# An attention and mixture-of-experts kernel: gate weights of the last token block moved from VectorE to GpSimd, and the waits of the first scatter-adds of each list put in another order

## The reference

```python
x = x + moe(layernorm(x))
# moe(h), h: 2048 x 256, 8 experts of width 512, the two best for each token
probs = softmax(h @ wg.T)
topk_w, topk_idx = top_k(probs, 2)
topk_w = topk_w / sum(topk_w)
y_e = (silu(h @ w1[e].T) * (h @ w3[e].T)) @ w2[e].T     # for each expert e
out = sum over the token's two experts of topk_w * y_e
```

## Time and profile before

| | us |
|---|---|
| median of 3 runs | 520.24 (519.79 to 520.38) |
| the profiled execution | 518.94 |
| its span, first to last instruction | 517.2 |
| TensorE busy | 497.2 (96%) |
| VectorE busy | 378.0 (73%) |
| ScalarE busy | 286.7 (55%) |
| GpSimd busy | 278.1 (54%) |

### The profile page before, as it was taken

How to read it: one execution, slowest core, us unless ns; L and a number is a source line. 1 busy time by engine, 2 the same in 40 slices (tenths; PEclk the granted TensorE clock), 3 DMA queues, 4 the chain that set the end, 5 groups by cost and what they waited for, 6 DMA issues and landing times.

```text
span 517.2 us, 11065 instructions
## 1 busy us (share of the span) xinstructions
PE 497.2 (96%) x3686; PEld 327.2 (63%) x3686; DVE 378.0 (73%) x984; ACT 286.7 (55%) x575; POOL 278.1 (54%) x312
## 2 busy tenths in 40 slices
PE   7899999999999999999999999999999999999992
PEld 3576766657566676666666676656666566666661
DVE  5898888577977659886888899998978544444441
ACT  3656777665656746584466757665454343444420
POOL 3563303002572705996298476355466576787554
PEclk9999999999999999999999999999999999999998
DMA  8002432436697626976579944245595779897763
GB/s 268 29 21 82 147 129 68 137 80 111 137 173 135 144 77 129 188 144 164 127 141 183 211 149 156 72 124 93 99 196 105 113 139 130 140 152 127 119 96 41
DMA packets 135337, 65.62 MB, mean 127 GB/s; under 512 B 109779, under 2 KB 126612, under 8 KB 135284
## 3 DMA queue, kind: packets, MB, share of 16 engines
q1 hardware_dynamic: 127796, 54.69, 48.4%
q0 software_dynamic: 7488, 10.23, 12.9%
HBM read 28.19 MB, written 10.35 MB: 75 GB/s over the span
## 4 chain that ended last, share of the span: by engine, by line
PE 58%; DVE 12%; DMA 9%; issue 7%; ACT 7%; POOL 3%; POOLq 2%; SPq 1%; DVEq 0%; ACTq 0%
PE ps L1224 47%; DMA out<-y,qst 3%; DMA probT<-prob 3%; PE ps L1319 3%; PE ps L1320 3%; PE ps L1321 3%; ACT ps L1033 2%; DVE cmax L1766 2%; POOL out L983 1%; DMA y<-hrow,qst 1%; ACT prob L1032 1%; ACT tT L1019 1%; DVE ps L2373 1%; PE ps L1233 1%; POOLq L973 1%
## 5 line engine op out<-in xcount | busy, mean ns | idle before, releaser
L1224 PE MATMUL ps<-arena,probT 128*128 128x256 f16 (+2 forms) x1092 | 179.9, 318 | 1.8 <-DMA probT<-prob 1.1
L1224 PEld LDWEIGHTS ps<-arena,probT 128*128 128x128 f16 (+1 forms) x1092 | 104.5, 97 | 58.3 <-issue 3.0
L983 POOL DMA_INDIRECT out<-y,qst x39 | 61.9, 1587 | 28.5 <-DVE y L2387 9.8
L1224 PE MATMUL ps<-arena,qT 128*128 128x512 f16 (+1 forms) x384 | 69.1, 332 | 1.0 <-DVE prob L1907 0.7
L1032 ACT ACTIVATE prob<-ps,nbias 128x512 f16<-128x512 f32 x64 | 39.0, 609 | 50.5 <-DVE nbias L1772 50.5
L1160 ACT ACTIVATE w1m<-ps 128x512 f32<-128x512 f32 x39 | 23.3, 598 | 73.0 <-PE ps L1224 73.0
L2373 DVE SCALAR_TENSOR_TENSOR ps<-ps,w1m 128x512 f32<-128x512 f32 x39 | 27.2, 698 | 43.6 <-ACT w1m L1160 41.9
L801 POOL TENSOR_TENSOR rstd<-veps,expo 128x1 f32<-128x1 f32 x16 | 9.0, 562 | 91.5 <-DVE veps L1801 91.5
L1224 PE MATMUL ps<-arena,tT 128*128 x468 | 57.2, 273 | 0.6 <-DVE tT L2485 0.6
L1224 PEld LDWEIGHTS ps<-arena,qT 128*128 128x128 f16 x384 | 32.5, 97 | 36.1 <-issue 1.7
L952 POOL DMA_INDIRECT y<-hrow,qst x39 | 41.0, 1052 | 24.1 <-DVE qst L2129 10.7
(11 more groups left out here) (245 smaller groups left out, 921.3 us busy)
## 6 DMA issues: line engine op xcount, KB each, us to landing
stage<-we_in SPq DMA_DIRECT2D x33, 256.0 KB, 3.1
prob<-we_in SPq DMA_DIRECT2D x15, 256.0 KB, 3.8
xin<-x_in SPq DMA_DIRECT2D x16, 128.0 KB, 2.6
out<-y SPq DMA_DIRECT2D x16, 128.0 KB, 2.3
hrow<-tT SPq DMA_DIRECT2D x4, 512.0 KB
y<-x_in SPq DMA_DIRECT2D x3, 512.0 KB, 7.3
stage<-z_in SPq DMA_DIRECT2D x4, 256.0 KB, 5.6
prob<-w_in SPq DMA_DIRECT2D x4, 256.0 KB, 3.3
```

The source lines that it names most:

```text
L983: g.indirect_dma_start(out[:rows_of(p), :], bass.IndirectOffsetOnAxis(ridx[:, n:n + 1], 0), ys[:, n % RING, :], None, compute_op=ALU.add). ...
L1224: r = t.matmul(o, lhs(a), rhs(b), start=first and n == 0, stop=last and n == 2)
```

## The change

Two edits. The weights of block 3 are worked out by GpSimd's `weigh`, directly behind `gates(3)`, and VectorE's copy of the function is gone. In `add(n)` for n = 1, 2, 3, 4, 9 and 17 the wait for the landing of add n-1 is put first, and a `gap` multiplication stands behind the waits for landings and ahead of the wait for `weighted(n)`. For the other adds the waits and the `gap` are as before.

```diff
             def add(n):
 
                 p = phase_of(n)
-                wait(pool, "x1_out", 16 * TB * PHASES[p][0])
                 alone = n <= RING or n == PHASES[p][1]
                 apart = n > PHASES[2][1] + 1
+                if n and alone:
+                    add_done(n - 1)
+                wait(pool, "x1_out", 16 * TB * PHASES[p][0])
                 if n > 2:
                     add_done(n - 3)
                 if n > 1 and (alone or n % RING == 1) and not apart:
                     add_done(n - 2)
                 if n and alone:
-                    add_done(n - 1)
+                    g.tensor_tensor(gap[:, n:n + 1], expo[:, 0:1], expo[:, 0:1], ALU.mult)
                 if not alone:
...
                 if n == LOGITS_AT - 4:
                     gates(NB - 1)
+                    weigh(NB - 1)
             add(NJ - 1)
...
-            def weigh(j):
-
-                b = slice(j * TB, (j + 1) * TB)
-                wait(dve, "r_exp", j + 1)
-                wait(dve, "r_val", j)
-                link(v.tensor_scalar(den[:], ex[:], 1.0, 1.0 / GS, ALU.add, ALU.mult))
-                link(v.reciprocal(gf[:, :, 0], den[:]))
-                link(v.tensor_tensor(gf[:, :, 1], ex[:], gf[:, :, 0], ALU.mult))
-                link(v.tensor_copy(vals[:, 1, b, :], gf))
-                v.tensor_tensor(vals[:, 2, b, :], gf, vals[:, 1, b, :], ALU.subtract).then_inc(sm["r_val"], 1)
...
                 if n == 12:
-                    weigh(j)
                     tiles_hot(2)
                     spread_vals(2, (0,))
```

## The result

The changed kernel is slower: 523.61 us median of 6 runs (522.84 to 525.07) against 520.01 (519.03 to 520.38), ratio 1.008 with a 95% interval of 1.0057 to 1.0102. The forecast was 520.5 us and no change that can be told. The profiled execution of the changed kernel took 523.72 us, span 521.6.

A forecast was written before the change was run, and what follows sets the result against it. TensorE was taken to bound the kernel; the 0.80 us won at the third list is lost again waiting for the gather of tile 17, net +0.3: 520.24 + 0.3 = 520.5 us, range 519.4 to 521.6.

The forecast's parts named there:

- What bounds the kernel, and where the two paths meet: TensorE, busy 96%; its path (410.16) and GpSimd's meet at tile 17's transposes, 410.33; 0.97 us within reach.
- VectorE without the weights: Before the third list: VectorE ends 1.07 us earlier, so TensorE's whole 0.80 us wait goes.
- GpSimd with the weights: Behind gates(3): weights cost GpSimd 2.21 us, adds 6 and 7 come 1.04 later, add 8 at 400.35 or 400.74.
- the case with the short `gap`: At add 8: gap lasts 0.19 us, add 8 at 400.35, add 9 at 405.77, 0.18 later than before.
- The small operation: At add 9: from landing to add takes 0.43 us instead of 0.90, giving back 0.47, between 0 and 0.56.
- the same shift: At tile 17's transposes: 0.3 earlier to 0.6 us later, taken as +0.3, carried unchanged to the end.
- The rivals: Held gap at add 8, chance 0.2; quicker landings, 0.17; small operation saving nothing, 0.13; remaining list wait, no own chance.
- The slower rival: At add 8: VectorE holds the gap until 401.08, add 9 1.1 us later, time 521.35; chance 0.2.
- the lock: VectorE instructions with two SBUF inputs block GpSimd's gap at add 8 until 401.08; add 8 at about 401.3.
- Its own sign: Wrong if add 9 starts before 405 or after 406.7, or TensorE waits at a place outside the rows.

The follow-up runs named there:

- run 2: Kernel before with the second edit alone (new wait order and gap), weights of block 3 left on VectorE: 519.99 against 520.51 us, ratio 0.9994.
- run 1: Changed kernel with the second edit undone, only the weights of block 3 moved to GpSimd: 523.44 against 520.51 us, ratio 1.005.
- run 5: Kernel before plus one GpSimd power operation between add 9 and the gather of tile 17: 521.82 against 518.98 us, ratio 1.0042.
- run 6: Changed kernel plus one GpSimd power operation between add 9 and the gather of tile 17: 521.78 against 518.98 us, ratio 1.0048.
- run 8: The changed kernel measured once more, nothing else altered: 524.67 against 518.58 us, ratio 1.0109; the profiled execution took 519.96.
- run 9: Changed kernel plus the GpSimd power operation before the gather of tile 17, a second time: 522.35 against 518.58 us, ratio 1.0057.
- run 3: Changed kernel, transposing DMA of tile 15 issued only after the gather of tile 17 landed: 520.90 against 520.51 us, ratio 1.0001.
- run 7: Changed kernel with the gather of tile 17 alone issued ahead of add 9: 520.49 against 518.98 us, ratio 1.0028.
- runs 8 to 11: Same chip, changed kernel: again 1.0109; with GpSimd power operation 1.0057; gathers 17 and 18 ahead of add 9 0.9972; that plus transpose of tile 15 held back 0.9977.
- run 4: Changed kernel with the gathers of tiles 17 and 18 allowed ahead of add 9: 519.69 against 520.51 us, ratio 0.998.

## Why the prediction was wrong

- **What bounds the kernel, and where the two paths meet.** Right: TensorE, and the transposes of tile 17.
- **VectorE without the weights.** Right: the third list lost its 0.80 us of wait.
- **GpSimd with the weights.** The price of the weights was right (2.21 us, 386.11 to 388.32), but the place of add 9 was hit by luck. Forecast was add 9 later by 0.18 in the case with the short `gap`; measured against `gates` it was 19.78 - 19.59 = 0.19 us. Two errors cancelled. Add 8 started 15.07 behind `gates`, where 14.35 was forecast: the gather of tile 14 started 0.59 behind the weights and not 0.20, the `gap` of add 7 took 0.68, and add 7 itself 2.20. And add 8 landed sooner (4.37 from its start to the `gap`, where 4.99 and 0.1 were assumed).
- **The small operation.** Right: in the chain GpSimd's wait for the landing ends at 404.48 and add 9 starts at 404.85, 0.37 us, forecast 0.43. Alone it showed no gain (run 2).
- **The step that failed:** "The gather of tile 17 follows in lockstep, 1.85 behind add 9 and 2.84 on its way". The 1.85 is 1.87. The 2.84 was taken as a property of the gather, and it is one of its neighbours: 6.15 in the changed kernel, 5.89 in run 1, 3.4 to 4.0 in runs 5, 6, 8 and 9, and 2.83 with the transpose held back (run 3). I had worked out when VectorE's chain would move forward and did not follow what SyncE issues from it. The activations' transposes stand in none of my rows.
- **Its second cost.** "From there on TensorE is without a wait until 506, so the same shift stands at the end" failed too, by the clock: in the wait of 4.91 it fell to 1.2 GHz, which cost 1.9 us more. The forecast had waits of up to 1.6 and no clock in it. The change of the profiled executions adds up: 4.91 - 0.17 for the gather, 1.9 for the clock, -0.80 for the list, and about -1.2 by which this execution was ahead before the stage began, together 4.6, against 521.6 - 517.2 = 4.4 of span.
- **The rivals.** All dealt with lateness of GpSimd, 0.65 to 1.6 us at most. The slower rival had the right side and the wrong mechanism; what looks like the lock shows at add 7, not at add 8. There the `gap` (394.32 to 395.00) lies beside `tiles_hot`, and the issue of the add (from 395.16) beside a `spread_vals`, both on VectorE:

```profile
394.07 0.88 DVE L2105 SCALAR_TENSOR_TENSOR probT<-qst 128x704 f16<-128x704 f32 x1
394.99 0.89 DVE L2115 TENSOR_TENSOR xin<-probT,vals 128x704 f16<-128x704 f16 x1
```

Against the 0.19 and 1.60 of others the two took some 1.1 us more together, and the shorter landing of add 8 gave the delay back. That VectorE held GpSimd up there is read from these times alone.

- **Its own sign.** The prediction called itself wrong if add 9 started before 405. It started at 404.85, but in an execution that was 0.9 ahead; by the distance from `gates` that sign didn't fail, and the wait of 4.91 where 0.6 to 1.6 was expected did.

The Trainium skill, page DMA: Bandwidth & Descriptors, section Issuing engines are not separate DMA queues, states that transfers started by different engines run on the same 16 DMA engines and interleave with each other. By that rule, the trace agrees: q0 and q1 share the windows of the changed kernel (0.06 and 0.14 MB in the first) and take turns in those of `before_spin` (0.01 and 0.26 MB, then 0.25 and 0.00).

Eight of the profiled executions side by side (us; the last column is the stretch of TensorE from the transposes of tile 17 to those of tile 18, 4.2 at full clock):

| execution | issue of gather 17, from that of transpose 15 | its way | TensorE's wait | stretch |
|---|---|---|---|---|
| kernel before | 1.35 ahead | 2.84 | 0.17 | 4.17 |
| `turn_late` | transpose held back | 2.83 | 1.34 | 4.19 |
| `after_again` | 0.26 ahead | 3.89 | 2.34 | 4.15 |
| changed kernel | 0.05 behind | 6.15 | 4.91 | 6.09 |
| `weights_only` | 0.14 behind | 5.89 | 4.76 | 6.33 |
| `before_spin` | 0.21 behind | 4.00 | 2.93 | 5.83 |
| `after_spin` | 0.70 behind | 3.42 | 2.84 | 5.52 |
| `after_spin_again` | 0.87 behind | 3.61 | 3.20 | 6.91 |

That the transpose makes the gather slow is shown by run 3. What stays open is how the engines share their time, and so how much it costs in one execution. Issued 0.14 us behind the transpose the gather took 5.89, and 0.21 behind it 4.00; the gather of tile 18 in run 7, 0.30 behind, took 5.5. More than the time between the issues must decide. Nor was the clock's part measured by an experiment of its own; it is read from the rows.

## What to carry to other kernels

A duration from issue to landing belongs to its neighbours in time. Before a saving moves one chain forward, list every DMA that this chain issues, and look at which other transfer with a close deadline it will meet. Where two transfers meet, put the one that is needed first ahead by order of issue, in an idle time that the issuing engine has anyway: on the chip of runs 8 to 11 one number in the order of gathers turned 1.1% more into 0.3% less (run 4, on another chip, could not tell its gain from none).

## What the runs showed of the hardware

- An indirect gather that took 2.83 us from issue to landing without a DMA transpose beside it took up to 6.15 us with one. Mixed, the two queues carried 0.41 MB in 3.0 us in the changed kernel and 0.54 in `after_again`; one after the other, 0.52 in `before_spin`. The transpose of one tile landed 3.0 to 6.5 us after its issue in these executions.
- An indirect DMA of GpSimd that waits for a landing itself (add 9) started 0.90 us after it, in the kernel before, `weights_only` and `before_spin` alike. Behind a one-column multiplication that takes the wait it started 0.34 to 0.37 us after it, in the changed kernel, `after_again`, `after_spin` and `turn_late`.
- In an idle time of 4.91 us TensorE's clock fell from 2.4 to 1.2 GHz, and it was still at 1.2 (granted 0.50) from 413.90 to 415.90, a window in which TensorE was busy throughout. The clock fell in the same way around idle times of 2.84, 2.90, 2.93, 3.20 and 4.76 us (`after_spin`, `gather_first`, `before_spin`, `after_spin_again`, `weights_only`), and not around those of 2.34 in `after_again`, 1.94 in `one_first` and 1.34 in `turn_late`.
